# Another order of the parts within a group of pairs, and all low parts of x made by GpSimd

## What is computed

```python
output = jnp.einsum('bni,io->bno', feature, weight)
q = jnp.einsum('bni,io->bno', feature, wq)
k = jnp.einsum('bni,io->bno', feature, wk)
alpha = jnp.einsum('bno,bmo->bnm', q, k)
alpha = jnp.maximum(alpha, 0.0) * (graph != 0).astype(alpha.dtype)
alpha = jax.nn.softmax(alpha, axis=1)
y = jnp.einsum('bnm,bmo->bno', alpha, output)
x = _layernorm(x + y, axis=-1)          # feature is x, graph is adj, all float32
```

## Time and profile before

| | |
|---|---|
| runs | 541.98, 539.29, 539.57 us; median 539.57 |
| profiled execution | 538.71 us, of which the span of its instructions is 536.9 |
| granted TensorE clock, mean | 0.997 |
| PE busy | 515.9 us, 96%, 3259 matmuls |
| DVE busy | 386.4 us, 72% |
| ACT busy | 321.1 us, 60% |
| POOL busy | 267.2 us, 50% |
| xt<-in_x_t | 64 transfers of 256 KB, 3.4 us from issue to landing |

### The profile page before, as it was taken

How to read it: one execution, slowest core, us unless ns; L and a number is a source line. 1 busy time by engine, 2 the same in 40 slices (tenths; PEclk the granted TensorE clock), 3 DMA queues, 4 the chain that set the end, 5 groups by cost and what they waited for, 6 DMA issues and landing times.

```text
span 536.9 us, 9927 instructions
## 1 busy us (share of the span) xinstructions
PE 515.9 (96%) x3259; PEld 466.1 (87%) x3259; DVE 386.4 (72%) x741; ACT 321.1 (60%) x745; POOL 267.2 (50%) x198
## 2 busy tenths in 40 slices
PE   8999999999999999999999999999999999999993
PEld 6889997898979988799978989789897998879993
DVE  4767745779568786588857796577956978656676
ACT  5666565385853856648554676538585385664663
POOL 0397964358525567148551495435852565710002
PEclk9999999999999999999999999999999999999998
DMA  7405231053600625025240344205260062302344
GB/s 268 163 0 197 83 132 43 21 155 120 235 20 20 215 85 208 20 81 185 105 175 20 117 155 160 95 20 183 90 234 20 23 211 104 150 1 74 122 156 156
DMA packets 30719, 62.05 MB, mean 116 GB/s; under 512 B 2032, under 2 KB 3056, under 8 KB 30704
## 3 DMA queue, kind: packets, MB, share of 16 engines
q1 hardware_dynamic: 30704, 61.87, 33.3%
HBM read 45.09 MB, written 16.78 MB: 115 GB/s over the span
## 4 chain that ended last, share of the span: by engine, by line
PE 84%; DVE 9%; issue 3%; ACT 2%; DMA 1%; POOL 0%; DVEq 0%; POOLq 0%; SPq 0%; ACTq 0%
PE o_bank L293 11%; PE o_bank L295 11%; PE o_bank L294 11%; PE chain L293 10%; PE chain L295 9%; PE chain L294 9%; PE bank_y L293 5%; PE bank_y L294 5%; PE bank_y L295 5%; DVE p_lo L1052 3%; DVE v_lo L979 3%; PE bank_z L293 2%; PE bank_z L295 2%; PE bank_z L294 2%; DVE parts L991 1%
## 5 line engine op out<-in xcount | busy, mean ns | idle before, releaser
L1349 POOL TENSOR_TENSOR s_lo<-xs,s_hi 128x512 fp32r<-128x512 f32 x60 | 87.7, 1480 | 49.4 <-ACT s_hi L668 49.0
L1344 POOL TENSOR_TENSOR a_lo<-xt,a_hi 128x512 fp32r<-128x512 f32 x42 | 59.9, 1434 | 46.1 <-ACT a_hi L660 46.1
L1354 POOL TENSOR_TENSOR rstd<-var_eps,minus_half 128x4 f32<-128x4 f32 x15 | 15.3, 1018 | 117.1 <-DVE var_eps L1076 117.1
L295 PE MATMUL o_bank<-t_hi,a_lo 128*128 128x256 f32 x256 | 72.4, 283 | 0.0
L294 PE MATMUL o_bank<-t_lo,a_hi 128*128 128x256 f32 x256 | 72.4, 283 | 0.0
L293 PE MATMUL o_bank<-t_hi,a_hi 128*128 128x256 f32 x256 | 72.4, 283 | 0.0
L1052 DVE SCALAR_TENSOR_TENSOR p_lo<-soft,inv_sum,p_hi 128x256 fp32r<-128x256 f32 x64 | 55.2, 881 | 17.8 <-ACT p_hi L747 17.8
L1340 POOL TENSOR_TENSOR xs<-xt 128x512 f32<-128x512 f32 x30 | 39.6, 1336 | 41.8 <-DMA xt<-in_x_t 23.9
L687 ACT COPY parts<-chain 128x256 f32<-128x256 f32 x90 | 33.3, 371 | 42.6 <-PE chain L295 41.5
L677 ACT COPY parts<-chain 128x512 f32<-128x512 f32 x42 | 24.7, 587 | 47.1 <-DVE v_lo L979 32.0
L293 PE MATMUL o_bank<-v_hi,p_hi 128*128 128x512 f32 (+1 forms) x132 | 50.7, 384 | 1.4 <-DVE soft L1035 1.4
(11 more groups left out here) (191 smaller groups left out, 1599.0 us busy)
## 6 DMA issues: line engine op xcount, KB each, us to landing
xt<-in_x_t SPq DMA_DIRECT2D x64, 256.0 KB, 3.4
xn<-in_x SPq DMA_DIRECT2D x16, 1024.0 KB, 5.3
out<-xn SPq DMA_DIRECT2D x15, 1024.0 KB, 4.3
adj<-in_adj_t SPq DMA_DIRECT2D x16, 512.0 KB, 6.0
xn<-in_w SPq DMA_DIRECT2D x4, 256.0 KB, 4.6
xn<-in_wq_t SPq DMA_DIRECT2D x4, 256.0 KB, 6.0
parts<-in_wk_t SPq DMA_DIRECT2D x4, 256.0 KB, 6.1
out<-xn SPq DMA_DIRECT2D x4, 256.0 KB, 2.0
```

The source lines that it names most:

```text
L295: return nc.tensor.matmul(dst, a[1], b[0], start=False, stop=last, skip_group_check=shared)
L1344: nc.gpsimd.tensor_tensor(a_lo[:, slot, u], xt[:, u], a_hi[:, slot, u].bitcast(F32), ALU.subtract).then_inc(a_lo_ready[slot], 1)
L1349: nc.gpsimd.tensor_tensor(s_lo[:, slot, s], xs[:, s], s_hi[:, slot, s].bitcast(F32), ALU.subtract).then_inc(s_lo_ready[slot], 1)
```

## The change

Two things. First, `split_b` is gone: GpSimd makes the low parts of A11 and A12 of slot 1 too, each right after ScalarE's high part, and the waits on them count `a_lo_ready[1]` in one order of four. Second, in the lists of ScalarE and VectorE parts stand in another order: at the head of a group `split_v` of A22 and A21 come ahead of `sum_t(A11, 0)`, and ScalarE's squares of y later; in the V stage of pair a the four `split_p` come early, and ScalarE's high parts of the next x after them; at the end of the program ScalarE's squares and VectorE's `variances` and first `normalise` come earlier. No other instruction is added or removed.

```diff
--- before.py
+++ after.py
@@ -37,10 +37,8 @@
 S1, S2, S3, S4 = range(4)
 S_SUMMED = {S3: 1, S1: 2, S2: 3, S4: 4}
 
-
 A_HI = ({A21: 1, A11: 2, A12: 3, A22: 4}, {A11: 1, A12: 2, A22: 3, A21: 4})
-A_LO = ({A21: 1, A11: 2, A12: 3, A22: 4}, {A22: 1, A21: 2})
-B_LO_FIRST = {A11: 1, A12: 2}
+A_LO = ({A21: 1, A11: 2, A12: 3, A22: 4}, {A11: 1, A12: 2, A22: 3, A21: 4})
 S_HI = ({S2: 1, S3: 2, S1: 3, S4: 4}, {S3: 1, S2: 2, S4: 3, S1: 4})
 S_LO = ({S2: 1, S3: 2, S1: 3, S4: 4}, {S3: 1, S2: 2, S1: 3, S4: 4})
 
@@ -176,7 +174,7 @@
         b12_copied = sem("b12_copied")
         gt_summed, gt_hi_ready, gt_lo_ready = sem("gt_summed"), sem("gt_hi_ready"), sem("gt_lo_ready")
 
-        a_hi_ready, a_lo_ready, b_lo_ready = sems("a_hi_ready"), sems("a_lo_ready"), sem("b_lo_ready")
+        a_hi_ready, a_lo_ready = sems("a_hi_ready"), sems("a_lo_ready")
         x_summed, s_hi_ready, s_lo_ready = sems("x_summed"), sems("s_hi_ready"), sems("s_lo_ready")
 
         t_filled, t_copied, t_summed, c12_copied = sem("t_filled"), sem("t_copied"), sem("t_summed"), sem("c12_copied")
@@ -208,10 +206,7 @@
             def load_a(i, u):
 
                 sp.wait_ge(x_summed[1], 4 * i - 4 + READ_BY[u])
-                if u in B_LO_FIRST:
-                    sp.wait_ge(b_lo_ready, 2 * i - 4 + B_LO_FIRST[u])
-                else:
-                    sp.wait_ge(a_lo_ready[1], 2 * i + A_LO[1][u])
+                sp.wait_ge(a_lo_ready[1], 4 * i - 4 + A_LO[1][u])
                 load_block(2 * i, u)
 
             def load_b(i, u):
@@ -334,10 +329,7 @@
 
                 def x_split(u):
                     pe.wait_ge(a_lo_ready[0], 4 * i + A_LO[0][u])
-                    if u in B_LO_FIRST:
-                        pe.wait_ge(b_lo_ready, 2 * i - 2 + B_LO_FIRST[u])
-                    else:
-                        pe.wait_ge(a_lo_ready[1], 2 * i + 2 + A_LO[1][u])
+                    pe.wait_ge(a_lo_ready[1], 4 * i + A_LO[1][u])
 
                 def xs_split(s):
                     pe.wait_ge(s_lo_ready[0], 4 * i - 4 + S_LO[0][s])
@@ -547,7 +539,7 @@
                 pe.wait_ge(t_lo_ready, 8 * i + 4 + T_LO[1][A12])
                 pe.wait_ge(masked, 4 * i + 1)
                 fill_scores(1, 0)
-                pe.wait_ge(a_lo_ready[1], 2 * i + 2 + A_LO[1][A21])
+                pe.wait_ge(a_lo_ready[1], 4 * i + A_LO[1][A21])
                 pe.wait_ge(t_lo_ready, 8 * i + 8)
                 pe.wait_ge(masked, 4 * i + 2)
                 fill_scores(1, 1)
@@ -762,20 +754,20 @@
                 a, b, z, y = 2 * i, 2 * i + 1, 2 * i - 1, 2 * i - 2
                 split_p(z, 0)
                 split_v(z, A22)
-                centred_squares(y, 0, 0)
+                split_s(i, 1, S2)
                 split_v(z, A21)
+                split_p(z, 1)
+                split_s(i, 1, S4)
                 copy_t(i, P1, 0)
-                split_s(i, 1, S2)
-                split_s(i, 1, S4)
                 copy_t(i, P1, 1)
                 split_s(i, 1, S1)
                 split_a(i, 1, A22)
-                split_p(z, 1)
                 split_p(z, 2)
+                split_p(z, 3)
+                centred_squares(y, 0, 0)
                 copy_t(i, P6, 0)
                 split_t_a(i, A11)
                 copy_t(i, P6, 1)
-                split_p(z, 3)
                 copy_t(i, P5, 0)
                 copy_t(i, P5, 1)
                 centred_squares(y, 0, 1)
@@ -799,30 +791,27 @@
                 exponent(a, 2)
                 copy_v(a, P6, 1)
                 exponent(a, 3)
+                split_p(a, 0)
                 copy_v(a, P5, 0)
                 copy_v(a, P5, 1)
-                split_p(a, 0)
-                if more:
-                    split_a(i + 1, 0, A21)
                 split_p(a, 1)
                 v_released(a)
                 split_v(a, A22)
+                split_p(a, 2)
+                split_v(a, A11)
+                split_p(a, 3)
                 if more:
+                    split_a(i + 1, 0, A21)
                     split_s(i + 1, 0, S2)
+                split_v(a, A12)
+                if more:
                     split_s(i + 1, 0, S3)
                     split_s(i + 1, 0, S1)
-                split_v(a, A11)
-                split_v(a, A12)
-                if more:
                     split_a(i + 1, 0, A11)
-                split_p(a, 2)
+                split_v(a, A21)
                 if more:
                     split_a(i + 1, 0, A12)
                     split_s(i + 1, 0, S4)
-                split_v(a, A21)
-                split_p(a, 3)
-
-                if more:
                     split_a(i + 1, 0, A22)
 
                 act.wait_ge(t_lo_ready, 8 * i + 4 + T_LO[1][A12])
@@ -851,24 +840,24 @@
                 for r in range(R):
                     exponent(p, r)
                 copy_v(p, P1, 0)
+                split_p(p, 0)
                 copy_v(p, P1, 1)
-                split_p(p, 0)
+                split_p(p, 1)
+                split_p(p, 2)
                 copy_v(p, P6, 0)
-                split_p(p, 1)
+                centred_squares(p - 1, 0, 0)
                 copy_v(p, P6, 1)
-                split_p(p, 2)
+                centred_squares(p - 1, 0, 1)
                 copy_v(p, P5, 0)
                 split_p(p, 3)
                 copy_v(p, P5, 1)
-                centred_squares(p - 1, 0, 0)
+                centred_squares(p - 1, 0, 2)
                 v_released(p)
                 split_v(p, A22)
-                centred_squares(p - 1, 0, 1)
+                centred_squares(p - 1, 0, 3)
                 split_v(p, A11)
                 split_v(p, A12)
-                centred_squares(p - 1, 0, 2)
                 split_v(p, A21)
-                centred_squares(p - 1, 0, 3)
                 for r in range(R):
                     centred_squares(p, 1, r, by_tile=True)
 
@@ -1021,10 +1010,6 @@
                 rows, j = slice(u // 2 * M, u // 2 * M + M), u % 2
                 rest(v_lo[:, rows, j], whole, v_hi[:, rows, j]).then_inc(v_lo_ready, 1)
 
-            def split_b(i, u):
-                dve.wait_ge(a_hi_ready[1], 4 * i + A_HI[1][u])
-                rest(a_lo[:, 1, u], xt[:, u], a_hi[:, 1, u]).then_inc(b_lo_ready, 1)
-
             def mask(p, g, first=False):
                 if g == 0:
                     dve.wait_ge(adj_loaded, 16 * p + 16)
@@ -1086,13 +1071,13 @@
                 a, b, z, y = 2 * i, 2 * i + 1, 2 * i - 1, 2 * i - 2
                 split_v(z, A11, V_AT[1])
                 sum_v(z, A21)
+                split_v(z, A22, V_AT[1])
+                split_v(z, A21, V_AT[1])
+                split_p(z, 0)
                 sum_t(i, A11, 0)
-                split_v(z, A22, V_AT[1])
-                split_p(z, 0)
+                split_p(z, 1)
                 sum_t(i, A11, 1)
-                split_p(z, 1)
                 split_p(z, 2)
-                split_v(z, A21, V_AT[1])
                 split_p(z, 3)
                 sum_t(i, A22, 0)
                 sum_t(i, A22, 1)
@@ -1124,18 +1109,18 @@
                 split_t_b(i, A22)
                 split_t_b(i, A21)
                 invert(a)
+                split_p(a, 0)
                 sum_v(a, A22)
-                split_p(a, 0)
+                split_p(a, 1)
                 sum_v(a, A11)
                 split_v(a, A22, V_AT[0])
-                split_p(a, 1)
+                split_p(a, 2)
                 split_v(a, A11, V_AT[0])
+                split_p(a, 3)
                 split_v(a, A12, V_AT[0])
                 sum_v(a, A21)
 
                 mask(b, 0)
-                split_p(a, 2)
-                split_p(a, 3)
                 split_v(a, A21, V_AT[0])
                 mask(b, 1)
                 residual(a, i, 0, 0)
@@ -1151,7 +1136,6 @@
                 normalise(z, 1, 1)
                 if more:
                     relu_max(b, 2)
-                    split_b(i + 1, A11)
                     relu_max(b, 3)
                 else:
                     invert(b)
@@ -1162,7 +1146,6 @@
                 if more:
                     sum_v(b, A22)
                     sum_v(b, A11)
-                    split_b(i + 1, A12)
                     invert(b)
                     split_v(b, A12, V_AT[1])
 
@@ -1273,10 +1256,8 @@
                 mask(1, g)
                 for r in range(g * M, (g + 1) * M):
                     relu_max(1, r)
-            split_b(1, A11)
             sum_v(1, A22)
             sum_v(1, A11)
-            split_b(1, A12)
             invert(1)
             split_v(1, A12, V_AT[1])
             with dve.Fori(1, GROUPS - 1) as i:
@@ -1308,11 +1289,12 @@
             sum_v(last, A11)
             split_v(last, A22, V_LAST)
             split_v(last, A11, V_LAST)
+            variances(last - 1)
             split_v(last, A12, V_LAST)
             sum_v(last, A21)
+            normalise(last - 1, 0, 0)
             split_v(last, A21, V_LAST)
-            variances(last - 1)
-            for r in range(R):
+            for r in range(1, R):
```

(4 more changed lines are left out.)

## The result

The changed kernel takes 524.26 us (median of four runs, 524.03 to 525.37). The kernel before, on the same chip, takes 539.43 (538.47 to 541.98). The ratio is 0.9709, with an interval of 0.9678 to 0.9741: 15.2 us faster by the medians. By the profiled executions the gain is 538.71 - 524.03 = 14.68 us, where my sum said 13.1.

A forecast was written before the change was run, and what follows sets the result against it. TensorE's own work (62.14 of 63.60 us a group) was taken as the bound. Gains 9.7 + 2.3 + 1.65 - 0.6 = 13.1 us took 538.71 to 525.6, plus 0.86 for the median: 526.5, range 524.5 to 530 (to 534.5 with A).

The forecast's parts named there:

- (1): Head of a group: splits moved into VectorE's idle 4.40 us close TensorE's hole at P5, 7 x 1.39 = 9.7 us.
- (2): V stage of pair a: split_p ahead of mask(b, 0) closes TensorE's hole on mask(b, 1), 6 x 0.39 = 2.3 us.
- (3): Two split_b, 0.69 us each, leave VectorE; GpSimd gains 2 x 1.29 us of work; no term in the sum.
- (4): V stage of pair b: sum_v(b, A22) comes even with P4's need; debit 0.1 us x 6 = 0.6.
- (5): End of the program: earlier squares and normalise let the first residual start sooner; gain 1.65 us, bounds 0 and 1.7.
- The 0.87 for a clear gain: Whole program: chance of a time under 536.9 us, faster by over the 2.7 us a measurement can tell.
- the forecast: Whole program: the main case, 526.5 us, own range 524.5 to 530, chance 0.62.
- A: Rival: one more turn lost per group, at the head or in pair b's V stage; 533.7 us, chance 0.19.
- C: Rival: the hole at P5 doesn't close, another need of P5 or P6 being equally late; 535.6 us, chance 0.06.
- the rest: Whole program: something not listed, half on each side, chance 0.06.
- B: Rival: GpSimd's chain becomes the bound, 3.3 to 4.7 us a group; 546 to 554 us, chance 0.07.
- hole 1: Head of a group: TensorE's P5 waits for ScalarE's copy_t(P6, 0), 1.39 us lost, once a group, 7 times.

The follow-up runs named there:

- e3: The kernel before with VectorE's split_v of A22 and A21 ahead of sum_t(A11, 0), ScalarE's list untouched: 528.97 us, ratio 0.9807.
- e6: The kernel before with split_v(z, A21) moved up by two split_p only: 536.49 us in one run.
- e4: The kernel before with the new order in the V stage of pair a alone, on ScalarE and VectorE: 535.89 us, ratio 0.9937.
- e1: The kernel before with GpSimd making the low parts of A11 and A12 of slot 1, old order kept: 539.02 us, ratio 0.9996.
- e8: The changed kernel with GpSimd making the low part of A22 of slot 0 twice, ahead of rstd: 526.11 us in one run.
- e5: The kernel before with the new order at the end of the program alone, on ScalarE and VectorE: 538.61 us, ratio 0.9964.
- e7: The changed kernel with GpSimd making the low part of A12 of slot 1 three times: 533.64 us in one run.
- e10: As e7, but with ScalarE's old order at the head of a group: 524.99 us in one run.

## Where the prediction was right, and which step failed

**(1), the head.** Right in mechanism and place. I had `split_v(A21)` done 5.2 us after the group's start, and it is done 4.6 after; `sum_t(A11, 0)` starts when I said, with 0.65 us to spare where my table had next to nothing, and the copy waits for TensorE. ScalarE's new order counted for nothing in the sum, and e3 shows that it is worth nothing.

**(2), the mask.** Right: no wait for it, and GpSimd's first `a_lo` at 241.18, where 246.4 less the 5.25 us won by then is 241.15.

**The price of a hole, in (1) and (2).** This is the step that failed. I took a hole as the gap in front of its first matmul and had every start behind it follow at its usual pace: 7 x 1.39 = 9.7 us and 6 x 0.39 = 2.3 us. The second matmul behind a hole starts late too, by 0.08 us (before, and e6), so the stages give back 7 x 1.48 = 10.4 and 6 x 0.48 = 2.9 us (e3 and e4): 13.2 for my 12.0. For the same reason a group takes 61.64 us, and not the 61.8 to 61.95 that I gave as a sign. Why the second matmul is late stays open. This term alone puts the time outside the range: my low end of 524.5 already had no debit in it, and with holes at their measured price it would have been 523.3; the smaller base (below) lies within the 1.4 us that it gave to the spread.

**(3), the move of two low parts.** Right as no gain and no cost (e1).

**(4), the debit of 0.6.** Wrong as well, in the path and not only in size. I had eight low parts of GpSimd take 11.6 us (246.4 to 258.0), and they take 10.7, so `rstd`, which I had at 252.75 on the clock of after, starts at 251.88. And I had allowed 2.7 us for the two normalises that meet GpSimd in the V stage of b; they took 2.28. So `sum_v(b, A22)` starts at 259.22 where I had 265.75 - 5.25 = 260.5. P4 isn't at a tie but has 1.4 us in hand at the sum, 1.1 at `rstd` (e8), and nothing was debited.

**(5), the end.** 1.65 foretold, 1.60 seen (1.61 from the last O on in e5 alone).

**The sum and the base.** Of the 14.68 - 13.1 = 1.6 us, 1.2 are the steps behind thirteen holes and 0.6 the debit; the program's start takes 0.2 back. The other 0.6 us of the miss are the base. I had added 0.86 us, by which the median before lay above its own profile; after, the two are 0.23 apart. The order-only kernel shows how loose this is: its profiled run took 525.85 us and the other three 523.58 to 523.87, and its T1 is 1.8 us later than the changed kernel's. The 0.87 for a clear gain is the forecast, A and C alone (0.62 + 0.19 + 0.06); the part of the rest that was to count in it is missing.

**The rivals.** A (one more lost turn a group) didn't happen, but e7 builds one like it: 1.59 us a group at the very place, 9.6 us in all from T1 on. Turns are lost in the changed kernel too: the two `split_v` of 264.50 take 2.89 us, where one of them is 0.68 alone. What decides is whether the slack ahead of TensorE, 1.6 and 1.1 us, takes them. By the exclusive lock of the Trainium skill (SBUF — State Buffer, the part on the engine ports) two longer holds a group spoke against this change. The trace agrees that one side stands while the other finishes, and shows that here none of it reached TensorE. B and C didn't come near: GpSimd is busy 34.68 of 61.64 us, and hole 1 closed in full.

## What to carry to other kernels

Look for the short instruction that the bound engine waits for through another engine's queue: one subtraction of 0.68 us, late in its engine's list, held a copy that TensorE needed, and moving it and the one before it into idle time ahead was worth 10 of 15 us with no work saved. Measure a hole from start to start, and on to the second instruction behind it. And load a place before calling it tight or safe: one or two repeated instructions told how far the next wait was (1.1 and 1.6 us for these loads), where a table of estimated starts was off by 1.3.

## What the runs showed that I had not expected

- Behind a hole of 1.39, 0.66 or 0.39 us the second matmul starts 0.31 us after the first in place of 0.23 (0.34 behind e7's hole of 1.44), and behind e8's of 0.26 it starts 0.22 after in place of 0.12. e10's list of waits shows none in the loop, and the starts still show such a step of 0.11.
- The spread between runs sits ahead of the loop. Over the profiles of all these kernels T1 lies between 77.5 and 80.4 us, while T1 to the end agrees within 0.1 us for kernels that wait alike (444.36, 444.37, 444.37 and 444.38; 459.28 and 459.36). One profile, compared from T1, told as much here as a median.
- Four output transfers issued closer together, and 1.2 us nearer to the one of 1024 KB ahead of them, landed 0.7 us later by the median: the DMA engines were busy for 0.99 of the time, and what VectorE had won was lost there.
